# The opening of a second attention: x of batches 0 and 1 projected in a row, keys of context 4 and the additions of expert results moved

## What is computed

```
x = x + tanh(g_xattn[0]) * L0_xattn(layernorm(x), ctx)     # 16 heads of 16, softmax over the queries
x = x + tanh(g_ffn[0])   * L0_ffn(layernorm(x))            # 8 experts, 2 per token
x = x + tanh(g_xattn[1]) * L1_xattn(layernorm(x), ctx)     # 16 heads of 16; own keys and context keys
x = x + tanh(g_ffn[1])   * L1_ffn(layernorm(x))            # shared expert, 15 routed, 3 per token
```

## Time and profile before

| | us |
|---|---|
| runs: median (lowest, highest) | 1251.21 (1250.08, 1251.69) |
| profiled execution, its own time | 1247.79 |
| its span | 1245.70 |
| TensorE busy | 1172.0 (94%) |
| VectorE busy | 597.1 (48%) |
| ACT busy | 477.6 (38%) |
| POOL busy | 390.7 (31%) |

### The profile page before, as it was taken

One profiled execution on the slowest core, in us unless ns is written; L12 is line 12 of the kernel. 1 busy time (PEld: TensorE's weight loads), 2 busy tenths in 40 slices (PEclk: granted clock), 3 DMA queues, 4 the chain that ended last, 5 costly groups with the idle time before them and its releaser, 6 DMA issues. The chain is left out here.

```text
span 1245.7 us, 29066 instructions
## 1 busy us (share of the span) xinstructions
PE 1172.0 (94%) x11367; PEld 901.1 (72%) x11367; DVE 597.1 (48%) x1432; ACT 477.6 (38%) x1130; POOL 390.7 (31%) x410
## 2 busy tenths in 40 slices
PE   6999999978999999977799999999988999999998
PEld 4767777756999999944466666667665579999985
DVE  5777777774211101165556665666656711121126
ACT  3545555522332333222444444444454223323311
POOL 3666666632322221131100110110112145555420
PEclk9999999968999999985899999999999999999999
DMA  6011111306999998540200100100000459999965
GB/s 180 26 34 34 35 34 52 100 14 239 377 328 321 332 326 321 185 138 1 85 14 14 32 20 14 32 8 3 8 9 14 153 173 357 344 359 357 343 222 169
DMA packets 64371, 180.92 MB, mean 145 GB/s; under 512 B 10156, under 2 KB 36588, under 8 KB 55788
## 3 DMA queue, kind: packets, MB, share of 16 engines
q1 hardware_dynamic: 55068, 156.40, 36.6%
q0 software_dynamic: 8064, 22.03, 4.9%
q10 hardware_dynamic: 1104, 0.64, 0.2%
HBM read 163.11 MB, written 15.93 MB: 144 GB/s over the span
## 5 line engine op out<-in xcount | busy, mean ns | idle before, releaser
L2219 ACT ACTIVATE ex_hT<-kept_psum,ex_w 128x128 f32<-128x128 f32 x464 | 132.3, 368 | 294.9 <-PE kept_psum L2274 294.9
L2274 PE MATMUL kept_psum<-ex_xT,ex_w 128*128 128x128 f32 x1856 | 222.6, 276 | 0.0
L2274 PEld LDWEIGHTS kept_psum<-ex_xT,ex_w 128*128 128x128 f32 x1856 | 215.8, 193 | 0.1
L2285 PE MATMUL kept_psum<-ex_w,ex_hT 128*128 128x256 f32 x928 | 213.9, 379 | 0.0
L2181 DVE TENSOR_TENSOR ex_yt<-kept_psum,ex_b 128x256 f32<-128x256 f32 x84 | 35.6, 424 | 353.9 <-PE kept_psum L2285 353.9
L2285 PEld LDWEIGHTS kept_psum<-ex_w,ex_hT 128*128 128x128 f32 x928 | 170.1, 190 | 19.7
L2147 POOL DMA_INDIRECT ex_results<-ex_yt,ex_to_row x84 | 82.8, 985 | 254.7 <-DVE ex_yt L2181 254.7
L1217 ACT ACTIVATE at_probs<-kept_psum 120x800 f32<-120x800 f32 (+2 forms) x128 | 101.1, 841 | 86.3 <-PE kept_psum L1378 86.3
L1067 DVE TENSOR_REDUCE at_negmax<-kept_psum 100x2 f32<-100x722 f32 x128 | 115.2, 900 | 0.0
L568 ACT ACTIVATE at_probs<-kept_psum 120x800 f32<-120x800 f32 (+1 forms) x96 | 80.0, 836 | 74.1 <-PE kept_psum L691 74.0
L410 DVE TENSOR_REDUCE at_negmax<-kept_psum 120x8 bf16<-120x800 f32 (+1 forms) x96 | 90.5, 984 | 24.0 <-PE kept_psum L682 23.6
(11 more groups left out here) (249 smaller groups left out, 1685.0 us busy)
## 6 DMA issues: line engine op xcount, KB each, us to landing
ex_w<-in_pack_in SPq DMA_DIRECT2D x32, 1028.0 KB, 6.0
ex_w<-in_pack_out SPq DMA_DIRECT2D x32, 1024.0 KB, 7.6
ex_w<-in_pack_in SPq DMA_DIRECT2D x52, 514.0 KB, 5.3
ex_w<-in_pack_out SPq DMA_DIRECT2D x52, 512.0 KB, 6.0
at_ctx<-in_ctxT SPq DMA_DIRECT2D x31, 361.0 KB, 3.8
ex_normed<-ex_xhat SPq DMA_DIRECT2D x16, 200.0 KB
ex_ways<-ex_results SPq DMA_DIRECT2D x6, 400.0 KB
ex_w<-ex_results SPq DMA_DIRECT2D x6, 400.0 KB
```

What stands on the lines that cost most here:

```text
L2219: last = act.activation(hT[t % N][:, c, :], ps_h[:, (t * U + u) % N, i * P:(i + 1) * P], ACT.Gelu, bias=w1[t % N][:, B1 + c:B1 + c + 1])
L2274: last = pe.matmul(ps_h[:, (t * U + u) % N, i * P:(i + 1) * P], w1[t % N][:, c * ff + f:c * ff + f + P], xT[t % N][:, c, :], start=(c == 0 ...
L2285: last = pe.matmul(ps_y[:, t % N, 0:D], hT[t % N][:, c, :], w2[t % N][:, c * D:(c + 1) * D], start=(c == 0), stop=(c == FC - 1))
```

## The change

It splits the first two loads of expert results, so that batches 0 and 1 come first, and makes them a layer-norm group of their own (`GROUPS`, `add_first`). It turns and projects x of both batches ahead of the steps, which now begin at -1. The key projections of context 4 go from the early part into step -1. In step 0 the first by-query unit goes ahead of `turn_max`. On VectorE the additions of group 2 go into step 0, behind the second maxima, and those of group 3 to the end of step 1. The hand-over follows one step later. Left out below are the index changes that follow from these.

```diff
+    GROUPS = [range(0, 2), range(2, GB)] + [range(g * GB, (g + 1) * GB) for g in range(1, NG)]
+    GROUP_OF = [g for g, bs in enumerate(GROUPS) for b in bs]
-    EARLY_KEYS = range(KC * early.AHEAD, KC * NK)
+    KEYED = NK - 1
+    EARLY_KEYS = range(KC * early.AHEAD, KC * KEYED)
+
+    def key_batch(t):
+        b = KEYED if t == -1 else t + NK - 1
+        return b if t and b < B else None
+
+    def x_batch(t):
+        return t + 2 if 0 <= t < B - 2 else None
+
...
-    STEPS = range(-2, B + 4)
-    ahead = [(n, b) for b in range(PRE) for n in ("value01", "value2")]
-    ring = ahead + [(n, t + off) for t in STEPS for n, off in (LIGHT_ORDER if t in LIGHT else ORDER) if on(t + off) and (n, t + off) not in ahead
-                    and not (n in ("key0", "key1") and t + off < NK) and not (n in ("value01", "value2") and t + off == PRE)]
+    STEPS = range(-1, B + 4)
+
+    def used(n, off, t):
+        b = key_batch(t) if n in ("key0", "key1") else x_batch(t) if n in ("xT", "own") else t + off
+        return b if b is not None and on(b) and not (n in ("value01", "value2") and b <= PRE) else None
+
+    opening = [(n, b) for b in range(PRE) for n in ("value01", "value2")] + [(n, b) for n in ("xT", "own") for b in range(2)]
+    ring = opening + [(n, used(n, off, t)) for t in STEPS for n, off in (LIGHT_ORDER if t in LIGHT else ORDER) if used(n, off, t) is not None]
...
-            if t == 1:
+            if t == 2:
                 fed.finished(sp)
...
+        root(0)
         fed.gpsimd(pool, 0)
-        root(0)
+        root(1)
         for g in range(1, NG):
             fed.gpsimd(pool, g)
         for b in range(B + 4):
-            if b == 1:
+            if b == 2:
                 second.clear(pool)
                 prep.fill(pool)
             if on(b):
                 bias_x(b)
                 if b % GB == 0 and b // GB + 1 < NG:
-                    root(b // GB + 1)
+                    root(b // GB + 2)
...
+            bs = GROUPS[g]
+            if g == 0:
+                fed.summed_first(dve)
+            elif g < 3:
+                fed.summed(dve, g - 1)
+            for b in bs:
...
+        fed.vector_first(dve)
+        moments(0)
         fed.vector(dve, 0)
-        moments(0)
         newton(0)
         normed(0)
         normed(1)
         take_values01(PRE)
         take_value2(PRE)
+        moments(1)
         fed.vector(dve, 1)
-            if t == 2:
+            if t == 3:
                 second.enter(dve)
...
+            if t == 0:
+                newton(1)
+                normed(2)
             if on(t + 1):
                 maxima(t + 1, 1)
...
-            if t == -2:
-                moments(1)
-            if t > 0 and t % GB == 1 and (t + 3) // GB + 1 < NG:
-                moments((t + 3) // GB + 1)
+            if t == 0:
+                fed.vector(dve, 2)
+            if t in (1, 2):
+                moments(t + 1)
+            if t == 5:
+                moments(4)
...
+            if t == 0:
+                normed(3)
+            if t == 1:
+                newton(2)
+                normed(4)
+            if t > 0 and on(t + 4):
                 if (t + 4) % GB == 0:
-                    newton((t + 4) // GB)
+                    newton((t + 4) // GB + 1)
                 normed(t + 4)
...
-            if t in (-1, 0):
-                fed.vector(dve, t + 3)
-            if t == 0:
+            if t == 1:
+                fed.vector(dve, 3)
                 fed.finished(dve)
                 second.leave(dve)
...
+        take_xT(0)
+        take_xT(1)
+        take_own(0)
         fed.scalar(act, 1)
+        take_own(1)
         for t in STEPS:
-            if t == 2:
+            if t == 3:
                 second.enter(act)
-            if on(t + NK - 1) and t > 0:
-                take_key(t + NK - 1, 0)
+            if key_batch(t) is not None:
...
-            if t < 0:
-                fed.scalar(act, t + 4)
             if t == -1:
+                fed.scalar(act, 2)
+                fed.scalar(act, 3)
                 second.leave(act)
...
-                if b < NK:
-                    pe.wait_ge(early.key_taken, KC * NK)
+                if b < KEYED:
+                    pe.wait_ge(early.key_taken, KC * KEYED)
                 else:
-                    pe.wait_ge(taken["key1"], b - NK + 1)
+                    pe.wait_ge(taken["key1"], b - KEYED + 1)
...
+        turn_x(0)
+        turn_x(1)
+        pe.wait_ge(w_loaded, 32)
+        project_own(0)
+        project_own(1)
         for t in STEPS:
-            if t == 2:
+            if t == 3:
...
-            if on(t):
+            if on(t) and t != 0:
                 turn_max(t)
             if on(t + 1):
                 by_query(t + 1, 0)
-            if on(t + NK - 1) and t > 0:
-                project_key(t + NK - 1, 0)
+            if t == 0:
+                turn_max(t)
+            if key_batch(t) is not None:
+                project_key(key_batch(t), 0)
...
+            if key_batch(t) is not None and t != -1:
+                project_key(key_batch(t), 1)
             if on(t + 1):
                 by_query(t + 1, 1)
+            if t == -1:
+                project_key(key_batch(t), 1)
...
+        FIRST = 0 if shared else 2
+        first_in = [] if shared else [m.sem(f"first_in{i}") for i in range(top)]
...
+
+            def load_way(i, j0, j1, loaded):
+                row = i % top * TOK + (i // top * GB + j0) * T
+                sp.dma_start(parts[i][:, j0:j1, :],
+                             ways[row:row + (j1 - j0) * T].rearrange("(b t) d -> t b d", t=T)).then_inc(loaded, 16)
+
+            for i, loaded in enumerate(first_in):
+                load_way(i, 0, FIRST, loaded)
             for i in range(NG * top):
-                g, way = i // top, i % top
-                row = way * TOK + g * GB * T
-                sp.dma_start(parts[i][:, :, :],
-                             ways[row:row + GB * T].rearrange("(b t) d -> t b d", t=T)).then_inc(ways_in[i], 16)
+                load_way(i, FIRST if i < top else 0, GB, ways_in[i])
...
+        def add_first(dve):
+            for i in range(top):
+                dve.wait_ge(first_in[i], 16)
+                need(dve, added, i * FIRST)
+                for b in range(FIRST):
+                    dve.scalar_tensor_tensor(out=xs[:, b, :], in0=parts[i][:, b, :], scalar=gates[:, i, b:b + 1], in1=xs[:, b, :],
+                                             op0=ALU.mult, op1=ALU.add).then_inc(added, 1)
+
         def add_ways(dve, g):
+            j0 = FIRST if g == 0 else 0
             for i in range(g * top, (g + 1) * top):
                 way = i % top
                 dve.wait_ge(ways_in[i], 16)
-                need(dve, added, i * (GB - 1) if way else 0)
-                for j in range(GB - 1):
+                need(dve, added, g * top * (GB - 1) + top * j0 + way * (GB - 1 - j0) if way else 0)
+                for j in range(j0, GB - 1):
                     b = g * GB + j
...
+
+        def summed_first(eng):
+            eng.wait_ge(added, top * FIRST)
```

More of the change, by code:

```diff
@@ L986, in root @@
         def root(g):
-            at = slice(g * GB, (g + 1) * GB)
+            bs = GROUPS[g]
+            at = slice(bs[0], bs[-1] + 1)
             pool.wait_ge(var_ready, g + 1)
-            pool.tensor_tensor(r0[:, at], var[:, at], mhalf[0:T, :].to_broadcast([T, GB]), ALU.pow).then_inc(root_ready, 1)
+            pool.tensor_tensor(r0[:, at], var[:, at], mhalf[0:T, :].to_broadcast([T, len(bs)]), ALU.pow).then_inc(root_ready, 1)
         def bias_x(b):
@@ L1027, in moments @@
         def moments(g):
-            if g < 2:
-                fed.summed(dve, g)
-            for b in range(g * GB, (g + 1) * GB):
+            bs = GROUPS[g]
+            if g == 0:
[3 more added lines that the diff above has]
+            for b in bs:
                 last = dve.bn_stats(stats[:, b, :], xs[:, b, :])
@@ L1053, in normed @@
         def normed(b):
-            dve.wait_ge(newton_step, 4 * (b // GB + 1))
+            dve.wait_ge(newton_step, 4 * (GROUP_OF[b] + 1))
             need(dve, ready["xT"], b - 1)
@@ L1252, in scalar @@
                 exponents(t, 1)
-            if on(t + 2):
-                take_xT(t + 2)
+            if x_batch(t) is not None:
+                take_xT(x_batch(t))
             if on(t - 1):
                 take_sum(t - 1, 1)
-            if on(t + 2) and t not in LIGHT:
-                take_own(t + 2)
+            if x_batch(t) is not None and t not in LIGHT:
+                take_own(x_batch(t))
             if B <= t <= B + 1:
                 prep.early_scalar(act, range(t - B, t - B + 1))
-            if t < 0:
-                fed.scalar(act, t + 4)
             if t == -1:
+                fed.scalar(act, 2)
+                fed.scalar(act, 3)
                 second.leave(act)
@@ L1266, in scalar @@
                 exponents(t, 2)
-            if on(t + 2) and t in LIGHT:
-                take_own(t + 2)
```

(20 more changed lines are left out.)

10 lines of the change are left out of this document (4 added, 6 removed).

## The result

The changed kernel takes 1239.69 us (median of 6 runs, 1235.15 to 1241.17) against 1250.64 for the kernel before in the same rounds (6 runs, 1249.54 to 1251.69): a ratio of 0.9907 [0.9892, 0.9922], 10.95 us faster. The forecast was 6.4 us faster, 1244.8.

A forecast was written before the change was run, and what follows sets the result against it. Steady steps bound by TensorE's work, the second attention's opening by a chain through all engines at half clock. Terms -11.25 + 1.8 - 1.65 + 2.65 + 2.0 = -6.45 took 1251.2 to 1244.8 us; range 1237 to 1250.

The forecast's parts named there:

- (a): Opening of second attention: split loads, fewer additions and statistics bring the first normalised x 3.6 us earlier, bounds 0 to 4.2.
- (b): Early part: moving out context 4's keys saves 2.5 us there; TensorE then waits 2.5 us for x instead of 3.61.
- (c): Row from first transpose to by-key of batch 0: by-key at 564.15 instead of 575.39, 11.25 us gained.
- (d): Clock falling at the wait before x: 1.8 us lost, bounds 0 and 2.7; falls in the row, step 0 largely half clock.
- (e): Step 0, by-key to by-key: 27.5 us instead of 29.16, gain 1.65, as group 3's additions no longer end it.
- (f): Group 3's additions ending step 1 delay by-key of step 2 by 2.65 us, plus 2.0 for a clock fall.
- (g): Moved moments, hand-over, second-expert loads, key copies and POOL's clearing: all at nothing; uncovered, the moments would cost 2.0 us.
- the clock holds: Rival: clock stays up through the maxima, step 0 takes at most 21.28 us; 15.3 to 17.3 us gained; chance 0.13.
- The first x comes no earlier: Rival: split transfers share the queue and land together, so only 1.95 us gained, 1249.3 us; chance 0.15.
- Slower through group 3's additions: Rival: additions stop TensorE in step 2 and the clock stays low; 25 us of it give 1254 us; chance 0.07.

The follow-up runs named there:

- whole_loads: Changed kernel with the two first ways of expert results loaded whole again, statistics of batches 0 and 1 kept apart: 1242.24 us, 0.9937 of the kernel before.
- gap_filled: Changed kernel plus two spare matmuls in TensorE's wait ahead of the first transpose of x: 1238.35 us, 0.9893 of the kernel before.
- warm: Changed kernel plus ten spare matmuls in TensorE's waits of the row of maxima, step 0 and step 1: 1231.03 us, 0.9837 of the kernel before.
- before_again: The kernel before, unchanged, run and profiled a second time: 1250.81 us, ratio 1.0002; its profiled execution took 1252.85 us.
- adds3_step0: Changed kernel with group 3's additions moved from the end of step 1 to step 0, behind the third maxima: 1234.34 us, 0.9865 of the kernel before.
- keys_early: Changed kernel with the key projections of context 4 back in the early part: 1238.15 us, 0.9899 of the kernel before.
- warm_adds3: Changed kernel plus spare matmuls in TensorE's waits and group 3's additions moved to step 0: 1228.66 us, 0.9810 of the kernel before.

## Why the prediction was right, and where its size was off

The direction held, and the mechanism up to the end of step 0; the forecast was 5.1 us too high. By its own steps:

- **(a) first x:** 3.99 us earlier, forecast 3.6. VectorE starts the sums 6.1 us after the first value projection, where the working has 6.2 (538.05), and does not wait for the second halves either, so these landed at least a little sooner than taken. The four additions took 1.86 us, where the working has 2.3: its 0.58 each is the mean of three, of which the third, batch 2's, takes 0.95 us and the two that were kept 0.48 each. `whole_loads` shows that the halves matter.
- **(b) wait before x:** 2.05 us, forecast 2.5.
- **(c) by-key of batch 0:** 10.79 us earlier, forecast 11.25 - 1.8 = 9.45. Of the 1.3 between them 0.4 is (a)'s and 0.6 is (d)'s; the row itself, from the first by-query unit to by-key, took 13.72 us where the working has 14.0.
- **(d) the early fall:** two projections took 5.41 us instead of the 3.79 of `gap_filled`, and the first by-query unit came 6.22 us after the first transpose instead of 5.05 there (18.05 - 13.00): 1.2 lost, charged at 1.8. The fall in the row, and step 0 at half clock, came as written; `warm` shows that the clock is what made it slow.
- **(e) step 0:** 27.49 us, forecast 27.5.
- **(f) group 3's additions:** the by-key unit of step 2 came 4.47 us later (12.46 to 7.99), forecast 2.65 + 2.0 = 4.65. That these agree is luck, for the parts are others. From by-key to by-key, step 1 takes 21.28 us in the execution that the prediction used. It takes 24.03 where the clock falls and no additions stand there (`before_again`, `adds3_step0`), 23.90 with the additions and no fall (`keys_early`), and 25.75 with both, here. So 2.75 us are a fall behind waits of 1.74 and 1.39 us that comes without the additions too, and the additions add 1.72; the wait was 1.70 and not 2.65 because with TensorE at half clock they ran beside work that took longer. Where the clock holds until there, as in `warm` and `keys_early`, it goes as forecast: a wait of 2.62, and a fall behind it, with which step 2 of `keys_early` takes 24.53 us instead of 22.87 (1.7, charged at 2.0).
- **(g)**, taken at nothing, is not clearly nothing. The steps from 3 on are unchanged, but another 0.85 us went between the by-key unit of step 2 and the turn of maxima 3 (7.99 to 7.14). It is not the additions': the by-key unit at 628.75 runs in pieces and takes 3.81 us to the next unit, where the kernel before took 2.97 (637.83 to 640.80). TensorE stops in it for 0.25 us (629.93), while the loads for the second experts, which the change puts into step 2, keep all 16 DMA engines busy (share 1.01 from 629.68 to 629.93). `warm` and `warm_adds3` stop likewise for 1.12 and 1.22 us, at shares of 0.73 and 1.09; `keys_early`, with the same loads in step 2, does not. No run takes the later loads back, so the cause stays open.

Together that is -7.14 us against -6.45 forecast: 0.7 off, with parts of (f) and (g) that are not those of the working. The step that failed is the one that put this sum on the median: "that execution lies 3.4 us low; I subtract the sum from the median". It supposes that the same sum holds for all executions. The execution read was one in which the clock survived the waits of step 1; `before_again` shows another in which it did not, 4.4 us longer by the turn of maxima 3, 2.75 of them by that fall. In the changed kernel's profile the clock falls there, and that execution (1239.54) lies at its median. So the sum charged the change for a fall that other executions of the kernel before pay as well. Of the 10.95 us, 7.14 are the change's steps in the two traces, 1.10 lie ahead of them, where nothing was changed, and 2.7 are the difference of how far each profiled execution lies below its median (2.85 and 0.15). That these 2.7 are clock falls is shown for one more execution, and there for the greater part, not for each.

Of the rivals, "the clock holds" was wrong for this kernel. Its 7.9 us for step 0 (29.16 to at most 21.28) cannot be set beside the 8.0 of `warm`, which count from 27.49: from 29.16 `warm` gains 9.7. "The first x comes no earlier" is refuted: it came 3.99 us earlier. "Slower through group 3's additions" had the place: moving them is worth 5.3 us by the medians, 2.3 of which the one trace of it shows; the rest stays open. Two parts of the change were not undone alone: the order of the first by-query unit and the turn in step 0, and the hand-over one step later.

## What to carry to other kernels

Before a sum is taken from one profiled execution, see whether that execution lies at the median, and whether a second one has the same clock in the same stretches; where the clock hangs on two short waits, the sum has two values. In a stretch that a chain of engines bounds, the clock can be worth nearly as much as the order of the work: here moving work gained 11 us and filling TensorE's waits with spare matmuls another 8.7, at no cost to the chain, since they end before the wait does. Work that an idle engine does for later goes into a wait that is there and not to the end of a step ahead of an instruction that others wait for.

## What the runs showed of the hardware

The same waits of TensorE let the clock fall in one execution and hold in another. Behind 1.39 and 1.34 us with a 1.03 us unit between them it fell in the changed kernel (557.04 and 559.42) and held in `gap_filled` (557.23 and 559.60); behind 1.74 and 1.39 it fell in `before_again` and held in the first profile of the same program, and the step took 24.03 us in the one and 21.28 in the other. Behind a wait of 2.62 us at full clock it fell in `warm` (607.60) and in `keys_early` (613.49). The low clock was worth 8.0 us in a step of 27.49 that waits on other engines much of the time. The runs of `warm` lie 1.3 us apart (5 runs) and those of the changed kernel 6.0 (6 runs); but those of `warm_adds3` lie 3.3 apart, so that filled waits make the times steadier is not shown.
